# Wide attention with its layer norm moved into VectorE's steps

## What is computed

```
x  = x + attention_b(layernorm(x))          # layer 2, "b0"
attention_b(u):
    q, k, v = split(u @ w_qkv)              # 32 heads of 32
    out     = softmax(q k^T / sqrt(32)) v
    y       = out @ w_out + b_out
    return (y - mean(y)) / sqrt(var(y) + 1e-6) * ln_gamma + ln_beta
x  = x + ffn(layernorm(x))                  # layer 3, mixture of experts, eps 1e-5
```

## Time and profile before

| what | value |
|---|---|
| runs | 4424.2, 4443.54, 4454.39 us, median 4443.54 |
| profiled execution | 4445.84 us, its span 4444.1 us |
| TensorE busy | 3459.6 us (78%) |
| VectorE busy | 3251.8 us (73%) |
| ScalarE busy | 2437.2 us (55%) |
| GpSimd busy | 1186.1 us (27%) |

### The profile page before, as it was taken

The page is one execution under the profiler, slowest core; times in us unless marked ns, Lnnn a source line. Parts: engine busy times, 40 slices in busy tenths (PEclk is TensorE's granted clock), DMA queues, the critical chain, the costliest instruction groups (busy, mean ns, idle before and its releaser), DMA issues. The chain is left out here.

```text
span 4444.1 us, 58108 instructions
## 1 busy us (share of the span) xinstructions
PE 3459.6 (78%) x18272; PEld 2097.8 (47%) x18272; DVE 3251.8 (73%) x7326; ACT 2437.2 (55%) x4422; POOL 1186.1 (27%) x732
## 2 busy tenths in 40 slices
PE   4888888539938999999999932994499998656736
PEld 2555555427724444455544422773266665422214
DVE  3999999427856777777777652786388886679986
ACT  2788888316724555565555511672299997312103
POOL 0000000051422555555555515142000000044520
PEclk9899999769967999999999965997799999878768
DMA  6333322112336565666665401132533332000000
GB/s 182 55 64 59 57 43 34 29 57 79 136 98 87 82 88 86 88 89 89 89 88 85 58 30 57 66 134 85 182 45 59 63 61 38 13 20 5 5 27 25
DMA packets 287843, 304.30 MB, mean 68 GB/s; under 512 B 98175, under 2 KB 187711, under 8 KB 287412
## 3 DMA queue, kind: packets, MB, share of 16 engines
q1 hardware_dynamic: 277812, 280.57, 33.8%
q0 software_dynamic: 9728, 20.01, 1.3%
HBM read 123.05 MB, written 75.72 MB: 45 GB/s over the span
## 5 line engine op out<-in xcount | busy, mean ns | idle before, releaser
L1042 DVE TENSOR_REDUCE at_b_top<-ps 128x1 f32<-128x512 f32 x1024 | 659.0, 678 | 313.5 <-PE ps L827 312.7
L956 ACT ACTIVATE at_b_e<-ps 128x512 f32<-128x512 f32 x1024 | 579.7, 598 | 484.2 <-PE ps L833 470.7
L731 POOL TENSOR_TENSOR at_b_e_pair<-at_b_e 128x1024 f32<-128x1024 f32 x256 | 601.4, 2382 | 539.5 <-PE ps L855 471.6
L549 ACT ACTIVATE at_a_e<-at_a_logits,at_a_neg_top 128x512 f32<-128x512 f32 x1024 | 656.1, 715 | 156.2 <-DVE at_a_neg_top L609 155.1
L473 PE MATMUL ps<-at_a_k,at_a_q 96*128 96x512 f32 x1024 | 477.2, 491 | 184.5 <-DVE at_a_clipped L577 117.4
L827 PE MATMUL ps<-at_b_k,at_b_q 96*128 96x512 f32 x1024 | 496.8, 489 | 27.4 <-DMA at_b_k<-at_b_k_hi 24.5
L542 ACT ACTIVATE at_a_eT<-ps 128x512 f32<-128x512 f32 x896 | 462.0, 589 | 0.4
L833 PE MATMUL ps<-at_b_q,at_b_k 98*128 98x512 f32 x1024 | 428.9, 420 | 19.2 <-ACT at_b_e L956 18.8
L605 DVE CUSTOM_DVE_ANT_0 at_a_logits<-ps,at_a_strip 128x512 f32<-128x512 f32 x512 | 340.4, 689 | 107.9 <-issue 33.1
L577 DVE TENSOR_SCALAR at_a_clipped<-ps 128x512 f32<-128x512 f32 x512 | 352.1, 688 | 39.8 <-PE ps L473 38.7
L473 PEld LDWEIGHTS ps<-at_a_k,at_a_q 96*128 96x128 f32 x1024 | 184.7, 190 | 396.4 <-DVE at_a_clipped L577 206.6
(11 more groups left out here) (331 smaller groups left out, 6542.6 us busy)
## 6 DMA issues: line engine op xcount, KB each, us to landing
moe_stage<-in_moe_w SPq DMA_DIRECT2D x46, 768.0 KB
at_b_q<-at_b_q_hi SPq DMA_DIRECT2D x128, 256.0 KB, 5.5
at_b_k<-at_b_k_hi SPq DMA_DIRECT2D x128, 256.0 KB, 6.1
v<-in_a_va SPq DMA_DIRECT2D x64, 256.0 KB, 3.6
at_a_v<-v SPq DMA_DIRECT2D x64, 256.0 KB, 7.0
at_b_q<-at_b_q_lo SPq DMA_DIRECT2D x64, 256.0 KB, 6.9
at_b_k<-at_b_k_lo SPq DMA_DIRECT2D x64, 256.0 KB, 6.8
slot_rows<-empty_slots SPq DMA_DIRECT2D x44, 258.0 KB, 6.8
```

The lines of the kernel that those rows point to most:

```text
L549: act.activation(e[:, j, qb, :], logits[:, j % 2, qb, :], ACT.Exp, bias=neg_top[:, j % 2, qb:qb + 1]).then_inc(exp_done, 1)
L731: pool.tensor_tensor(e_pair[:, j, :, :], e[r][:, j, 0:2, :], e[r][:, j, 2:4, :], ALU.add).then_inc(pair_done, 1)
L956: act.activation(e[r][:, j, b, :], g.ps[:, ST_BANK + b % 2, :], ACT.Exp).then_inc(exp_done, 1)
L1042: dve.tensor_reduce(top[:, t, j, qb:qb + 1], g.ps[:, bank, :], AX_X, ALU.max).then_inc(max_done, 1)
```

## The change

The bias stays where it was. What followed in two phases of their own is cut into 37 parts (`LN_PARTS`), with 51 VectorE instructions to a batch, and each part but the first waits for the part before it. One part is put at the end of each slot in the three steps after a batch's bias: parts 0 to 15 in the slots of step 6, 16 to 31 in those of step 7, 32 to 36 in slots 0 to 4 of step 8. For the last batch the 37 parts come after the steps, at a stretch. The instructions of the reciprocal root now have 4 columns in place of 32, and are issued for each batch. The store of y, its load and two phases go; two loads (gamma and beta) join those that the attention waits for at its start. `rsqrt_part` returns the k-th of the 12 instructions of the root.

The parts of a batch: 0 and 1 two `bn_stats` each, 2 four `bn_aggr`, 3 a copy of the variance, 4 to 15 the root (4, 5 and 6 with one input; 7, 10 and 13 `tensor_tensor`; 8, 9, 11, 12, 14 and 15 `scalar_tensor_tensor`); 16 and 17 two (y - mean) * gamma each; 18 and 19 two * rstd + beta each; 20 the sum with x; 21 to 36 the statistics of x, as 0 to 15.

```diff
-def attend_wide(nc, g, name, scale):
+def attend_wide(nc, g, name, scale, gamma, beta):
...
+        RS_LINKS = RSQRT_LINKS
+        LN_PARTS = 2 * (RS_LINKS + 4) + 5
+        LN_COUNT = 2 * (RS_LINKS + 2 * TB + 1) + 2 * TB + 1
...
+                for k, vec in enumerate((gamma, beta)):
+                    sp.dma_start(gb[:, k, :], vec[None, :].to_broadcast([P, DM])).then_inc(w_loaded, 16)
...
-                    if st.c == 5 and st.has(5):
-                        sp.wait_ge(y_added, st.i)
-                        settle(sp, sp_settled)
-                        sp.dma_start(item(g.y_dram, st.i).rearrange("b p n -> p (b n)"),
-                                     y_tok[:].rearrange("p t d -> p (t d)")).then_inc(y_stored, 16)
...
+                def stats_part(k, data, mv, rstd, eps):
+                    if k < 2:
+                        for tb in range(2 * k, 2 * k + 2):
+                            dve.bn_stats(y_stats[:, tb, :], data[:, tb, :]).then_inc(ln_done, 1)
+                        return 2
+                    if k == 2:
+                        for tb in range(TB):
+                            dve.bn_aggr(mv[:, tb, :], y_stats[:, tb, :]).then_inc(ln_done, 1)
+                        return TB
+                    if k == 3:
+                        dve.tensor_copy(y_var[:], mv[:, :, 1]).then_inc(ln_done, 1)
+                    else:
+                        rsqrt_part(dve, k - 4, y_var[:], eps, rstd, y_t[:]).then_inc(ln_done, 1)
+                    return 1
...
+                def layer_norm(b, k):
+                    x = g.x_all[:, (b - 1) * TB:b * TB, :]
+                    if k == 0:
+                        dve.wait_ge(y_added, b)
+                    wait(dve, ln_done, LN_COUNT * (b - 1) + ln_counts[k])
+                    first = RS_LINKS + 4
+                    if k < first:
+                        stats_part(k, y_tok, y_mv, y_r[:], 1e-6)
+                    elif k < first + 2:
+                        for tb in range(2 * (k - first), 2 * (k - first) + 2):
+                            dve.scalar_tensor_tensor(y_tok[:, tb, :], y_tok[:, tb, :], y_mv[:, tb, 0:1], gb[:, 0, :],
+                                                     ALU.subtract, ALU.mult).then_inc(ln_done, 1)
+                    elif k < first + 4:
+                        for tb in range(2 * (k - first - 2), 2 * (k - first - 2) + 2):
+                            dve.scalar_tensor_tensor(y_tok[:, tb, :], y_tok[:, tb, :], y_r[:, tb:tb + 1], gb[:, 1, :],
+                                                     ALU.mult, ALU.add).then_inc(ln_done, 1)
+                    elif k == first + 4:
+                        dve.tensor_tensor(x, x, y_tok[:], ALU.add).then_inc(ln_done, 1)
+                    else:
+                        stats_part(k - first - 5, x, g.mean_var[:, (b - 1) * TB:b * TB, :],
+                                   g.rstd[:, (b - 1) * TB:b * TB], 1e-5)
...
+                            if st.c >= 6 and st.has(5) and st.i >= 1 and 4 * j + qb + 16 * (st.c - 6) < LN_PARTS:
+                                layer_norm(st.i, 4 * j + qb + 16 * (st.c - 6))
                             if (j, qb) == (3, 2) and st.has(4):
                                 turn_l(st)
...
                 run(dve, step)
+                for k in range(LN_PARTS):
+                    layer_norm(B, k)
+                dve.wait_ge(ln_done, LN_COUNT * B)
...
-            attend_wide(nc, g, "at_b0", 32 ** -0.5)
-            add_normalised(nc, g, "ln_b0", g.y_dram, a["b0_gamma"], a["b0_beta"], 1e-6)
+            attend_wide(nc, g, "at_b0", 32 ** -0.5, a["b0_gamma"], a["b0_beta"])
+            g.stats_ready = True
```

More of the change, by code:

```diff
@@ L138, in rsqrt, with rsqrt_part @@
         link(dve.scalar_tensor_tensor(y, t, 1.5, y, ALU.add, ALU.mult))
+def rsqrt_part(dve, k, var, eps, y, t):
+    if k == 0:
+        return dve.tensor_scalar(var, var, eps, None, ALU.add)
+    if k == 1:
+        return dve.tensor_scalar(t.bitcast(I32), var.bitcast(I32), 1, None, ALU.logical_shift_right)
+    if k == 2:
+        return dve.tensor_scalar(y.bitcast(I32), t.bitcast(I32), -1.0, float(0x5F3759DF), ALU.mult, ALU.add)
+    if k % 3 == 0:
+        return dve.tensor_tensor(t, y, y, ALU.mult)
+    if k % 3 == 1:
+        return dve.scalar_tensor_tensor(t, t, -0.5, var, ALU.mult, ALU.mult)
+    return dve.scalar_tensor_tensor(y, t, 1.5, y, ALU.add, ALU.mult)
 def row_stats(nc, name, x_all, mean_var, rstd, eps, stats=None):
@@ L677, in attend_wide @@
         y_tok = ph.sb("y_tok", [P, TB, DM])
-        sp_settled = ph.sem("sp_settled")
+        gb = ph.sb("gb", [P, 2, DM])
+        y_stats = ph.sb("y_stats", [P, TB, 6])
+        y_mv = ph.sb("y_mv", [P, TB, 2])
+        y_var, y_t, y_r = (ph.sb(k, [P, TB]) for k in ("y_var", "y_t", "y_r"))
+        sp_settled, ln_done = (ph.sem(k) for k in ("sp_settled", "ln_done"))
         set_up, w_loaded = ph.sem("set_up"), ph.sem("w_loaded")
@@ L688, in attend_wide @@
                                 "pair_done", "pv_done", "o_copied"))
-        sums_done, l_turned, recip_done, r_done, o_done, y_ready, y_added, y_stored = (
-            ph.sem(k) for k in ("sums_done", "l_turned", "recip_done", "r_done", "o_done", "y_ready", "y_added",
-                                "y_stored"))
+        sums_done, l_turned, recip_done, r_done, o_done, y_ready, y_added = (
+            ph.sem(k) for k in ("sums_done", "l_turned", "recip_done", "r_done", "o_done", "y_ready", "y_added"))
         S_BANK, ST_BANK, PV_BANK, PROJ_BANK, Y_BANK = 0, 3, 5, 6, 7
+        RS_LINKS = RSQRT_LINKS
+        LN_PARTS = 2 * (RS_LINKS + 4) + 5
+        LN_COUNT = 2 * (RS_LINKS + 2 * TB + 1) + 2 * TB + 1
         RS = 3
@@ L771, in step @@
                             sp.dma_start(k4[r][row:row + 32].bitcast(F32), src[:].bitcast(F32)).then_inc(loaded[r], 16)
-                    if st.c == 5 and st.has(5):
-                        sp.wait_ge(y_added, st.i)
-                        settle(sp, sp_settled)
-                        sp.dma_start(item(g.y_dram, st.i).rearrange("b p n -> p (b n)"),
-                                     y_tok[:].rearrange("p t d -> p (t d)")).then_inc(y_stored, 16)
                 run(sp, step)
-                sp.wait_ge(y_stored, 16 * B)
             @block.tensor
@@ L784, in _ @@
                 pe.wait_ge(set_up, RQ + 1)
-                pe.wait_ge(w_loaded, 16 * (U + 2))
+                pe.wait_ge(w_loaded, 16 * (U + 4))
                 def turn_x(batch):
@@ L1001, in add_bias @@
                     dve.wait_ge(y_ready, U * st.i)
-                    wait(dve, y_stored, 16 * (st.i - 1))
+                    wait(dve, ln_done, LN_COUNT * (st.i - 1))
                     dve.tensor_tensor(y_tok[:], g.ps[:, Y_BANK, :].rearrange("p (t d) -> p t d", t=TB),
                                       bias[:, None, :].to_broadcast([P, TB, DM]), ALU.add).then_inc(y_added, 1)
+                def stats_part(k, data, mv, rstd, eps):
[3 more added lines that the diff above has]
+                        return 2
+                    if k == 2:
+                        for tb in range(TB):
[6 more added lines that the diff above has]
+                    return 1
@@ new lines, in _ @@
+                ln_counts = [0]
+                for k in range(LN_PARTS):
+                    part = k if k < RS_LINKS + 4 else k - RS_LINKS - 9
+                    ln_counts.append(ln_counts[-1] + (2 if 0 <= part < 2 else TB if part == 2 else 1 if part >= 0 else
+                                                      1 if part == -1 else 2))
+                assert ln_counts[-1] == LN_COUNT
+                def layer_norm(b, k):
+                    x = g.x_all[:, (b - 1) * TB:b * TB, :]
+                    if k == 0:
+                        dve.wait_ge(y_added, b)
[16 more added lines that the diff above has]
+                                   g.rstd[:, (b - 1) * TB:b * TB], 1e-5)
@@ L1029, in _ @@
                 dve.memset(ones[:], 1.0).then_inc(set_up, 1)
-                dve.wait_ge(w_loaded, 16 * (U + 2))
+                dve.wait_ge(w_loaded, 16 * (U + 4))
                 def step(st):
```

## The result

The changed kernel takes 4495.49 us (median of four runs, 4490.39 to 4495.74) against 4448.97 us (median of four, the three runs known before among them). The ratio is **1.0112, 95% interval 1.0077 to 1.0147**. The forecast was 4520 us with a range of 4445 to 4580. The profiled execution has 4495.74 us, 49.9 more than that of before, where 74 were forecast.

A forecast was written before the change was run, and what follows sets the result against it. TensorE, busy 143.8 of 150 us in steady attention, was taken to set the pace. The profiled 4445.8 - 41.6 (removal net of start) + 102 (steps) + 14 (clock) = 4520 us, range 4445 to 4580.

The forecast's parts named there:

- The first rival: The gain alone: VectorE's free 4.3 us a step take all the parts, 4404 us; chance 8%.
- the second: No stands: in the steps only VectorE's own time counts, 29 us in all, 4433 us; chance 14%.
- The removal: Between last bias and mixture: mixture begins at 2599.2 instead of 2641.9, 42.7 us saved.
- The tail's 11.3 us: After the last bias: the last batch's 37 parts in a row take 11.3 us.
- the exit's 3.3: After the last batch's parts: semaphores and barrier before the mixture, 3.1 to 3.4 us.
- The start's 1.1 us: Two broadcast loads ahead of all work lose 1.1 us, bounds 0 and 3.
- The steps: Steps 6 to 8: parts standing behind GpSimd delay TensorE, 14.6 us a batch, +102 for seven.
- the missed ends: Waiting VectorE instructions miss a GpSimd instruction's end with 0.30 chance; 0.8 us for each of two windows a batch.
- the row I preferred: L1018, 0.17 us shortest, 0.685 median, up to 3.6: read as missing a GpSimd end in 0.30 of steps.
- own pitch: VectorE's own time per instruction in the slots: 0.2 us a small part, 0.6 a reduction, L1012 or large transpose.
- One sign: TensorE's waits for the maxima and the low part of k rise by some 100 us in total.
- The clock: Slower granted clock in 14 windows of the affected steps: 1 us each, 14 us, bounds 0 and 56.

The follow-up runs named there:

- at slot 1: The kernel before with the low part of the maxima (L1018) at the end of slot 1 in place of slot 2: ratio 0.9948.
- the fifth experiment: The kernel before with L1018 and its transpose moved from slots 2 and 3 to 6 and 7, SyncE's row copies behind those of k: ratio 0.991.
- the version with slots 6 to 15: The changed kernel with the 37 parts in slots 6 to 15 of steps 6, 7, 8 and 1: ratio 1.012 to the kernel before.

## Why the prediction came out as it did

**The direction and the mechanism were right.** "By that average they are free. By slots they are not": the run with one-input instructions, the run in GpSimd's idle slots and the run without GpSimd's reads show it from three sides. What stands is a little more than the prediction said: see the last section. The first rival (4404) is the number of the removal alone, the second (4433, no stands) that of the one-input run, which gave 0.995 where 0.997 was forecast. Both were right in size and wrong in their condition.

**The removal**: forecast 42.7 us, measured 42.5. The tail's 11.3 us were 11.4, the exit's 3.3 were 3.45. The start's 1.1 us for two more loads was 0.1: the first bias sum comes at 1561.85 instead of 1561.71, so the lower bound was the right value.

**The steps**, forecast 102 and measured 94 with the clock in it. By step, as the interval that ends at the low part of k, mean of seven batches:

| step | before | after | growth | forecast |
|---|---|---|---|---|
| 6 | 17.85 | 20.04 | 2.2 | 2.0 |
| 7 | 18.50 | 24.48 | 6.0 | 7.6 |
| 8 | 18.74 | 22.55 | 3.8 | 5.0 |
| 1, next batch | 19.08 | 20.20 | 1.1 | 0 |
| 2 to 5 | 75.59 | 75.65 | 0.1 | 0 |
| batch | 149.8 | 162.9 | 13.1 | 14.6 |

The clearest mis-sized term is the missed ends. I had taken 0.30 from L1018 and added 0.8 us for each of two runs; of the 56 instructions of the parts that stood in this kernel none missed an end. Without the two terms the forecast is 6.8 for step 7 and 4.2 for step 8. There the page "SBUF — State Buffer" of the Trainium skill, section "SBUF: two separate sides", in the reading that the next in wait gets the ports, fitted the parts better than the row I preferred. It does not fit L1018, neither in the kernel before nor at slot 1. The rest is own pitch: the low part of k was done 17.0 us into the first run and not 18.0, and 14.7 into the second (1765.88 to 1780.60) and not 15.8, since a small part takes 0.16 us by its row but holds the next one up by 0.08 only (in slot 2 of step 7 L1082 starts at 1752.09, the part behind it at 1752.17); I had counted 0.2. The 1.1 us of step 1 I had not forecast. A part of it is L1018's successor, L1082: in three of the seven it came 7.1 to 7.4 us into the run, past the third end, and stood to the fourth. The rest is not traced.

Step 6 came out near its forecast by another way than I had given. I had L1082 pushed to 7.4 us, past the third end, in every batch. My own row shows VectorE idle for 1.06 us ahead of slot 2, and this took up most of the two parts: L1082 came at 6.56 us. In four of seven batches it missed the third end, and in three it did not, and then the copy of slot 3 stood to the fourth end in its place. The start and duration of L1082 in one batch of each kind (its runs of GpSimd begin at 1720.89 and 1885.98), and the copy in the first:

```profile
1727.44 0.52 DVE L1082 SCALAR_TENSOR_TENSOR at_b_tops<-at_b_top,at_b_tops 128x16 fp32r<-128x16 f32 x1
...
1728.88 1.43 DVE L1035 COPY at_b_y_var<-at_b_y_mv 128x4 f32<-128x4 f32 x1
...
1892.54 2.88 DVE L1082 SCALAR_TENSOR_TENSOR at_b_tops<-at_b_top,at_b_tops 128x16 fp32r<-128x16 f32 x1
```

So the 2.2 us by 2.0 are in part luck.

One sign did not come as forecast. TensorE's waits for the maxima and the low part of k were to rise by some 100 us. Its weight loads waited 95.2 us for the maxima instead of 79.8, its matmuls 23.0 for the low part of k instead of 13.5. TensorE's new waits come before slot 5 and are for two other results, twice a batch each (total us, times, longest):

```profile
PE ps L860 <- DVE at_b_r_sb L1002: 23.7, 14, 1.7
...
PE ps L835 <- DVE at_b_k_lo L1076: 23.0, 25, 1.1
PE ps L822 <- DVE at_b_q_lo L1076: 18.5, 14, 2.5
```

The prediction followed VectorE's lateness to slot 5 alone. The two new waits are 42 us of TensorE's idle time; that for the low part of k rose by 9.5.

**The clock**: forecast 14 us in bounds of 0 to 56. The falls came, 16 of them, two and sometimes three a batch. In the two batches with a third fall, step 7 took 25.0 and 25.3 us, and 24.2 to 24.3 in the others: 0.8 to 1.0 us for a fall that nothing hides. As an estimate, if no fall costs more than that, 16 of them are at most 13 to 16 us. How much of the 94 they are was not measured by itself.

**The forecast of 4520** was 24 us too high for the profiled execution: 22 too many in the steps and the clock together (116 forecast, 94 measured), 1 at the start, and 2 from what follows the attention. Of the 22, the missed ends that no part missed are 11 (14 windows at 0.8). The pitch, about 1 us a window, is some 15 more; against them stand the 8 us of step 1 that I had not forecast. The few that are left are not traced. The direction and the stands held; what was off is the size of these terms, and where in the step TensorE waits.

**The order of slots was under-used.** With L1018 at slot 2 the kernel before already carried a loss of the same kind, 39 us on the chip of the fifth experiment. The row that priced the change also named an improvement that did not need it.

## What to carry to other kernels

Before work goes into an engine's idle time, look at what its neighbours do in those slots: on VectorE an instruction with two SBUF inputs stands still while GpSimd runs one that reads SBUF, up to the end of the neighbour's instruction, at times of the one after it, and once for each instruction, however few its columns. A copy and a scalar instruction of 4 columns stood too. Put such instructions where GpSimd is idle (37 parts at no cost, against 94 us at the wrong slots), and look for those that already stand: a line whose longest duration is many times its shortest.

## Seen of the hardware

- A copy of four columns, with one input, stood as well. One line of the changed kernel (ns min/median/max):

```profile
L1035 DVE COPY at_b_y_var<-at_b_y_mv x8: 120/145/1432, 1568.9 to 2680.3; 128x4 f32<-128x4 f32 x8
```

Three of the eight met a run of GpSimd's and took 1.43 us each. I had counted parts with one input as free. The Trainium skill, page "SBUF — State Buffer", section "Who interferes with whom", says that a copy can take the shared ports as well, in a two-port mode; the trace agrees that a copy can stand, at 1.43 us.
- A `tensor_scalar` of four columns, with one input, stood too. In the version with slots 6 to 15 the first instruction of the root that writes `rstd` took 1.52 us in each of the seven batches, and 0.17 in the tail (ns min/median/max):

```profile
L148 DVE TENSOR_SCALAR rstd<-at_b_y_t x8: 170/1517/1519, 1574.3 to 2645.2; 128x4 int32<-128x4 int32 x8
```

- Reductions out of SBUF (0.14 us for 4 columns) and `bn_stats` (at most 0.29 us) did not stand in the same slots.
- An instruction that arrives at the change from one GpSimd instruction to the next passes in 0.11 us; one that arrives 0.6 us later waited 4.16 us.
